# Sliding-window attention with experts on Trainium2: scores of two head pairs over 32 rows each, interleaved, and a block moved from behind the experts to the front

## Chip, cores and metric

One core of one Trainium2 chip runs the whole program. The metric is the device time of one execution in microseconds, the median of several runs.

## What is computed

The input x is 4 x 1024 tokens of 256 values, taken here as 32 blocks of 128 tokens. After a layer norm, three things are added to x: a gated mix of windowed and latent attention, a mixture of experts, and a shared expert.

```python
# per head (16 heads of 16): window of 128 keys behind each query
scores = einsum('bhnqd,bhnkd->bhnqk', qb, kb) * scale
attn = softmax(where(allowed, scores, NEG))
local = einsum('bhnqk,bhnkd->bhnqd', attn, vb)
# latent: 64 pooled tokens a batch, 4 heads of 16
lattn = softmax(where(lat_allowed, rq @ rk.T * lscale, NEG))
remote = (lattn @ rv) @ rout_w + rout_b
gate = sigmoid(local @ gl_w + remote_h @ gr_w)
attention = (gate * local + (1 - gate) * remote_h) @ out_w + out_b
# experts: top 8 of 64 for each token, and a shared one
y = sum_k w[k] * (silu(x @ We_gate[e_k]) * (x @ We_up[e_k])) @ We_down[e_k]
return x + attention + y + (silu(xn @ Ws_gate) * (xn @ Ws_up)) @ Ws_down
```

## The kernel before

Everything is float32, and the order on each engine is written out by hand; engines meet through counting semaphores only. The program runs in four stages: layer norm and routing; a first attention over blocks 0 to 16 (`FIRST` = 17); the experts, 96 pairs of tiles of 128 rows; and a second attention over blocks 17 to 31.

**One block of attention** is `body`, written once for each engine with eight steps `s` = 0 to 7, one for each pair of heads. In step s TensorE (PE) computes the scores of pair s (`scores`, line 824), transposes the probabilities of pair s-2 (`turn_probs`, line 838) and multiplies those of pair s-3 with the values (`values`, lines 850 to 852). VectorE (DVE) adds the mask, takes the minimum and writes the negated scores to `sm` (`mask_pair`, line 1544); ScalarE (ACT) takes the exponentials (`exps`, line 1116) and copies the transposed probabilities out of PSUM (`keep_prT`, line 1124). The other work is spread over the steps: projections (lines 771, 782, 784), the shared expert (792), the latent attention (`latent_scores` 858, `latent_turn` 864, `latent_values` 870), the gate (`mix_sums`, `mix`), and the output projection (811, 812). Steps of the block before (`tail`) are finished in the first steps of the next.

**Scores of a pair.** Queries lie transposed in `qT`, 8 heads of 16 rows on the 128 partitions of one half c. `keep_q` on DVE (line 1487) multiplies them by `own_head` and writes eight copies to `qz`, in each of which only one head's 16 rows are not zero. So the scores of a head come from a product over all 128 rows of `kT`:

```python
for u in range(2):
    last = mm(psS[:, p % 2, u * WIN:(u + 1) * WIN], qz[:, c, u, heads, :].rearrange("p h t -> p (h t)"),
              kT[:, c, u * UQ:u * UQ + WIN], start=True, stop=True)
```

One such product stands in the trace as two MATMUL and two LDWEIGHTS instructions. `psS` has two banks; pair p uses bank p % 2 and waits until DVE has masked pair p-2. `sm` and `pr` have four places, and `psT[:, 0]`, to which the probabilities are transposed, one: `turn_probs` waits for `keep_prT` of the pair before.

**The latent steps** of a block: PE `latent_scores` in step 4, DVE `latent_max` in step 5, ACT `latent_exp` in step 6 (ahead of `keep_prT` and `exps` of that step), PE `latent_turn`, ACT `keep_lprT`, PE `latent_values` in step 7.

**Scatter.** While the first attention runs, GpSimd (POOL) sends the normed rows of all 32 blocks to their experts' slots in DRAM: 256 indirect DMAs at line 636, in order, paced not to run ahead of PE. Before the experts begin, ACT waits for `attention(0, FIRST)` on its own queue and then for all of these to land; its first loads of expert rows are at line 1232.

**Combine.** In the second attention DVE also adds the experts' rows, 8 for a token, so 8 instructions at line 1604 for each of 32 blocks, each waiting for the one before (`combine`). Rows come in by DMA into four places (`rows_in`), of which SP refills one when its block is combined. Before: 16 adds in steps 4 to 7 of the first block behind (`resuming`), 16 in each of the other 14 (`combining`), 16 after the last block's steps (`closing`).

## Time and profile before

| | us |
|---|---|
| median of 3 runs | 1334.67 (1333.65 to 1336.95) |
| the profiled execution, its time | 1338.67 |
| its span in the profile | 1336.9 |
| PE busy | 1255.4 |
| DVE busy | 953.3 |
| ACT busy | 861.7 |
| POOL busy | 638.7 |

Of the span, routing takes about the first 105 us, the first attention from there to 478 us, the experts to 993 us, the second attention the rest. Times in rows are microseconds from the start of the span, durations of one instruction in groups are nanoseconds. What stands in square brackets behind a row is how long the engine was idle before it, and who released it. Ends of matmuls are modelled, and each lasts longer than the distance to the next: the work of PE is read from the distance between starts.

### The profile page before, as it was taken

The page shows a single profiled execution, that of the slowest core. Times are in us where ns is not written, and L with a number is a line of the kernel's source. Part 1 is how long each engine was busy: PE and PEld are TensorE (multiplying, and loading weights), DVE is VectorE, ACT ScalarE, POOL GpSimd, SP SyncE. Part 2 cuts the span into 40 slices and gives each one's busy share as a digit, 9 for nine tenths or more (in the row PEclk, how much of TensorE's full clock was granted, in tenths as well). Part 3 has the DMA queues.
Part 4 walks back from the last instruction along what each step waited for, and adds up shares of the span by engine and source line. Part 5 has one row for each costly group of instructions (what it writes and reads, how often), then busy time and mean ns, then how long its engine had stood idle before and what let it go on. Part 6 is the DMA issues. An engine that isn't in the chain of part 4 may idle for free.

```text
span 1336.9 us, 38681 instructions
## 1 busy us (share of the span) xinstructions
PE 1255.4 (94%) x9266; PEld 1182.4 (88%) x9267; DVE 953.3 (71%) x4532; ACT 861.7 (64%) x2383; POOL 638.7 (48%) x747
## 2 busy tenths in 40 slices
PE   4957999999999989999999999999999999999996
PEld 3956999999999979999999999999988999999985
DVE  6776666666666637667676676765559898989897
ACT  2323877777777856556565566566657777777774
POOL 7803777777777726565565665656650000000000
PEclk9678999999999979999999999999999999999998
DMA  8107455544333337777777777775545333333330
GB/s 255 63 1 280 163 185 188 206 163 162 123 118 112 114 120 223 211 233 223 224 232 212 233 226 214 233 215 170 175 139 218 107 106 106 106 109 113 116 119 19
DMA packets 152813, 218.40 MB, mean 163 GB/s; under 512 B 24769, under 2 KB 124866, under 8 KB 147650
## 3 DMA queue, kind: packets, MB, share of 16 engines
q1 hardware_dynamic: 80450, 86.77, 20.4%
q0 software_dynamic: 28800, 86.54, 16.9%
q10 hardware_dynamic: 43520, 44.57, 13.1%
q8 instruction: 19, 0.31, 0.1%
q14 instruction: 24, 0.20, 0.0%
HBM read 113.86 MB, written 103.81 MB: 163 GB/s over the span
## 4 chain that ended last, share of the span: by engine, by line
PE 73%; DVE 12%; issue 6%; DMA 3%; ACTq 2%; ACT 2%; DVEq 1%; SPq 1%
PE psS L951 19%; PE psS L824 10%; PE psT L935 5%; PE psO L960 5%; PE psT L838 4%; PE psM L960 4%; DVE x_all L1604 4%; DMA pr<-slot_rows 2%; PE psQ L771 2%; PE psV L811 2%; PE psV L782 2%; PE psQ L792 2%; PE psT L852 2%; PE psT L851 2%; PE psT L850 1%
## 5 line engine op out<-in xcount | busy, mean ns | idle before, releaser
L951 PEld LDWEIGHTS psS<-sm,wt 128*128 128x128 f32 x2560 | 310.8, 193 | 19.5 <-issue 7.8
L951 PE MATMUL psS<-sm,wt 128*128 128x128 f32 x2560 | 316.6, 277 | 1.7 <-ACT sm L1210 0.7
L636 POOL DMA_INDIRECT slot_rows<-x_out_st,idx_st x256 | 257.0, 1004 | 77.5 <-issue 68.6
L1116 ACT ACTIVATE pr<-sm,nmax 128x192 f32<-128x192 f32 x512 | 205.1, 449 | 54.5 <-DVE nmax L1544 52.7
L824 PE MATMUL psS<-kT,qz 128*128 128x192 f32 x1024 | 225.2, 343 | 10.8 <-DVE qz L1487 8.4
L663 POOL DMA_INDIRECT home_rows<-qz,row_idx x160 | 154.6, 966 | 131.0 <-DVE qz L1637 103.4
L663 POOL DMA_INDIRECT home_rows<-sm,row_idx x160 | 155.3, 971 | 86.4 <-issue 45.0
L1228 ACT COPY wt<-shared_mem 128x512 f32 x320 | 183.4, 627 | 4.8 <-issue 4.8
L1216 ACT ACTIVATE prT<-psS 128x256 f32<-128x256 f32 x160 | 61.6, 385 | 187.7 <-issue 100.0
L824 PEld LDWEIGHTS psS<-kT,qz 128*128 128x128 f32 x1024 | 164.3, 192 | 18.4 <-issue 10.3
L1544 DVE CUSTOM_DVE_ANT_0 sm<-psS,pr 128x192 f32<-128x192 f32 x512 | 162.0, 353 | 18.5 <-issue 14.6
L1124 ACT COPY prT<-psT 128x384 f32<-128x384 f32 x256 | 121.9, 476 | 77.6 <-PE psT L838 74.1
L1630 DVE TENSOR_TENSOR prT<-psS,prT 128x256 f32<-128x256 f32 x160 | 67.7, 423 | 105.3 <-ACT prT L1216 102.3
L838 PE MATMUL psT<-ident,pr 128*128 128x128 f32 x768 | 126.2, 273 | 1.3 <-ACT prT L1124 1.2
L1604 DVE SCALAR_TENSOR_TENSOR x_all<-shared_mem,w,x_all (+1 forms) x256 | 122.8, 480 | 1.1
L838 PEld LDWEIGHTS psT<-ident,pr 128*128 128x128 f32 x768 | 100.1, 142 | 7.7 <-issue 1.9
L1210 ACT COPY sm<-psT 128x512 f32<-128x512 f32 x160 | 93.6, 585 | 10.1 <-PE psT L935 5.4
L1542 DVE MEMSET met<- 1x1 f32 x256 | 15.1, 59 | 104.4 <-PE psS L824 93.8
L1487 DVE TENSOR_TENSOR qz<-qT,own_head 128x1024 f32<-128x1024 f32 x64 | 78.2, 1221 | 6.9 <-ACT qT L1050 6.9
L960 PE MATMUL psO<-shared_mem,prT 128*128 x320 | 82.4, 380 | 0.2 <-DVE prT L1630 0.2
L960 PE MATMUL psM<-shared_mem,prT 128*128 x320 | 82.3, 380 | 0.0
L935 PE MATMUL psT<-ident,pr 128*128 128x128 f32 x480 | 74.3, 279 | 4.4 <-DMA pr<-slot_rows 2.3
(283 smaller groups left out, 2492.6 us busy)
## 6 DMA issues: line engine op xcount, KB each, us to landing
shared_mem<-home_rows SPq DMA_DIRECT2D x32, 1024.0 KB, 5.1
pr<-slot_rows ACTq DMA_DIRECT2D x120, 272.0 KB
qz<-slot_rows ACTq DMA_DIRECT2D x40, 272.0 KB
slot_rows<-wt SPq DMA_DIRECT2D x32, 272.0 KB
shared_mem<-in_L_ffn_We_gate SPq DMA_DIRECT2D x64, 128.0 KB
shared_mem<-in_L_ffn_We_up SPq DMA_DIRECT2D x64, 128.0 KB
shared_mem<-in_L_ffn_We_down SPq DMA_DIRECT2D x64, 128.0 KB
x_all<-in_L_attn_x SPq DMA_DIRECT2D x4, 1024.0 KB, 9.1
```

Of the source, the lines that this page charges most:

```text
L636: pool.indirect_dma_start(slot_rows, bass.IndirectOffsetOnAxis(ap=idx_st[:, j, k:k + 1], axis=0), x_out_st[:, j % 2, :], None).then_inc(sc ...
L663: pool.indirect_dma_start(home_rows, bass.IndirectOffsetOnAxis(ap=row_idx[:, j, a:a + 1], axis=0), ys[j][:, a, :], None).then_inc(y_out[j] ...
L824: last = mm(psS[:, p % 2, u * WIN:(u + 1) * WIN], qz[:, c, u, heads, :].rearrange("p h t -> p (h t)"), kT[:, c, u * UQ:u * UQ + WIN], star ...
L838: last = nc.tensor.transpose(psT[:, 0, a * P:(a + 1) * P], flat[:, a * P:(a + 1) * P], ident[:])
L935: last = nc.tensor.transpose(psT[:, j % 2, (a * DC + c) * P:(a * DC + c + 1) * P], xs[j][:, a, c * P:(c + 1) * P], ident[:])
L951: last = mm(psS[:, j % 2, (2 * a + n) * P:(2 * a + n + 1) * P], wt[j % 2][:, a, c, n * F:(n + 1) * F], xsT[:, j % 2, a, c, :], start=(c == ...
L960: last = mm((psM, psO)[j % 2][:, a * D:(a + 1) * D], hT[:, j % 2, a, :], ring_d[:, e % RING, :], start=True, stop=True)
L1116: nc.scalar.activation(pr[:, p % 4, par, :], sm[:, p % 4, par, :], ACT.Exp, bias=nmax[:, p % 4, par:par + 1], scale=-1.0).then_inc(probs, 1)
L1124: nc.scalar.copy(prT[:, p % 2].rearrange("p a t -> p (a t)"), psT[:, 0, 0:3 * P]).then_inc(prT_ready, 1)
L1228: last = nc.scalar.copy(wt[j % 2][:, a, :, :], ring_gu[:, e % RING, :, :])
L1544: v.tensor_tensor_reduce(sm[:, p % 4, u, :], psS[:, p % 2, u * WIN:(u + 1) * WIN], mask[:, u * WIN:(u + 1) * WIN], -1.0, -FLOOR, ALU.add, ...
L1604: ins = v.scalar_tensor_tensor(x_all[:, t, :], row, w8[:, t, k:k + 1], x_all[:, t, :], ALU.mult, ALU.add)
```

## The change

1. **Scores.** In the first attention alone (`two = start == 0`), PE takes the scores of pairs s and s+1 together in each even step. Each product now runs over the 32 rows of its own pair. The order is: keys' half u = 0 of pair s, of pair s+1, then u = 1 of both; two neighbours have other rows of the array and another bank of `psS`. It waits until DVE has masked all pairs before s. DVE masks both in the even step.
2. **Queries.** `keep_q` writes two copies of 128 columns, by `own_half` (two sums on POOL before the first attention), in place of eight.
3. **Latent steps**, first attention alone: `latent_scores`, `latent_max`, `latent_exp`, `latent_turn` and `keep_lprT` one step sooner; `latent_values` stays in step 7, but ahead of `values`.
4. **Blocks.** `FIRST` is 18: 18 blocks in front of the experts, 14 behind. The adds of line 1604 are dealt out anew: 24 in steps 4 to 7 of the first block behind, 16 in each of the other 13, and 24 after the last block's steps (3 in each step).

```diff
-FIRST = NB // 2 + 1
+FIRST = NB // 2 + 2
...
+            after(nc.gpsimd.tensor_tensor(own_quarter[:], own_head[:, 0:4], own_head[:, 4:8], ALU.add))
+            after(nc.gpsimd.tensor_tensor(own_half[:], own_quarter[:, 0:2], own_quarter[:, 2:4], ALU.add))
...
+            def scores_of_two(i, p, nth):
+                n = i * NPAIR + p
+                c = p // PPC
+                if p % PPC == 0:
+                    pe.wait_ge(q_kept, DC * i + c + 1)
+                    pe.wait_ge(k_kept, DC * i + c + 1)
+                if p or nth:
+                    pe.wait_ge(masked, 2 * n)
+                for u in range(2):
+                    for m in (p, p + 1):
+                        r = slice(m % PPC * 2 * HD, (m % PPC + 1) * 2 * HD)
+                        last = mm(psS[:, m % 2, u * WIN:(u + 1) * WIN], qz[r, c, u, 0:2, :].rearrange("p h t -> p (h t)"),
+                                  kT[r, c, u * UQ:u * UQ + WIN], start=True, stop=True)
+                        if u == 1:
+                            last.then_inc(s_ready, 1)
...
-                    if live:
+                    if live and two and s % 2 == 0:
+                        scores_of_two(i, s, nth)
+                    if live and not two:
                         scores(i, s, nth)
...
-                    if s == 7 and live:
+                    if s == 7 and live and early:
+                        latent_values(i)
+                    if s == 7 - early and live:
                         latent_turn(i)
...
-                    if s == 4 and live:
+                    if s == 4 - early and live:
                         latent_scores(i, nth)
...
-                    if s == 6 and live:
+                    if s == 6 - early and live:
                         latent_exp(i, nth)
...
-                v.tensor_tensor(qz[:, c, :, :, :], bcast(qT[:, c, :].rearrange("p (u t) -> p u t", u=2), HPC, 2),
-                                bcast(bcast(own_head[:], UQ, 2), 2, 1), ALU.mult).then_inc(q_kept, 1)
+                n, own = (2, own_half) if two else (HPC, own_head)
+                v.tensor_tensor(qz[:, c, :, 0:n, :], bcast(qT[:, c, :].rearrange("p (u t) -> p u t", u=2), n, 2),
+                                bcast(bcast(own[:], UQ, 2), 2, 1), ALU.mult).then_inc(q_kept, 1)
...
-                    if live:
+                    if live and two and s % 2 == 0:
                         mask_pair(i, s, nth)
-                    if closing and s in (1, 2, 5, 7):
-                        n = (1, 2, 5, 7).index(s)
-                        if n == 0:
-                            dve.wait_ge(acc_done, NB - 1)
-                        combine(NB - 2 + n // 2, 2 + n // 2, range(n % 2 * 4, n % 2 * 4 + 4))
+                        mask_pair(i, s + 1, nth)
+                    if live and not two:
+                        mask_pair(i, s, nth)
+                    if closing:
+                        for n in range(3 * s, 3 * s + 3):
+                            if n == K:
+                                dve.wait_ge(acc_done, NB - 1)
+                            combine(NB - 3 + n // K, (NB - 3 + n // K) % ROWS, (n % K,))
...
-                    if s == 5 and live:
+                    if s == 5 - early and live:
                         latent_max(i, blk)
...
-                combine(2 * (i - FIRST) + n // K, 2 * ((i + 1) % 2) + n // K, (n % K,))
+                combine(2 * (i - FIRST) + 1 + n // K, 2 * ((i + n // K) % 2) + 1 - n // K, (n % K,))
```

**PE, loop of the first attention, steps 6 and 7.** In the rows that follow, ISA and REGISTER_ALU rows are addresses and waits. Before:

```order
L821 ISA
L824 MATMUL psS<-kT,qz 128x192 x2
L833 REGISTER_ALU
L838 MATMUL psT<-ident,pr 128x128 x3
L850 MATMUL psO<-v_mid,prT 128x72
L851 MATMUL psO<-va,prT 128x36
L852 MATMUL psO<-va,prT 128x36
L821 ISA
L824 MATMUL psS<-kT,qz 128x192 x2
L833 REGISTER_ALU
L838 MATMUL psT<-ident,pr 128x128 x3
L864 MATMUL psM<-ident,lpr 128x128 x2
```

and of the changed kernel, the same place:

```order
L839 ISA
L843 MATMUL psS<-kT,qz 128x192 x4
L853 REGISTER_ALU
L858 MATMUL psT<-ident,pr 128x128 x3
L884 MATMUL psM<-ident,lpr 128x128 x2
L870 MATMUL psT<-v_mid,prT 128x72
L871 MATMUL psT<-va,prT 128x36
L872 MATMUL psT<-va,prT 128x36
L853 ISA
L858 MATMUL psT<-ident,pr 128x128 x3
L890 ISA
L890 MATMUL psM<-rv,lprT 128x34
```

The two groups of scores are one of four products, and the latent transpose has moved from step 7 to step 6.

**ACT, loop of the first attention, steps 5 and 6.** `tz` is the gate's tanh. Before:

```order
L1044 COPY kT<-kT 128x128
L1124 COPY prT<-psT 128x384
L1115 ISA
L1116 ACTIVATE pr<-sm,nmax 128x192
L1115 REGISTER_ALU
L1116 ACTIVATE pr<-sm,nmax 128x192
L1095 ACTIVATE tz<-z 128x16
L1130 ACTIVATE lpr<-small 128x256
L1124 COPY prT<-psT 128x384
```

and now:

```order
L1070 COPY kT<-kT 128x128
L1156 ACTIVATE lpr<-small 128x256
L1150 COPY prT<-psT 128x384
L1141 ISA
L1142 ACTIVATE pr<-sm,nmax 128x192
L1141 REGISTER_ALU
L1142 ACTIVATE pr<-sm,nmax 128x192
L1121 ACTIVATE tz<-z 128x16
L1150 COPY prT<-psT 128x384
```

The latent exponential (`lpr`) stands ahead of the copy and the exponentials of step 5.

**DVE, end of the second attention.** `x_all<-psV` is the sum of a block's attention into x, `x_all<-shared_mem` the adds of experts' rows. Before:

```order
L1604 SCALAR_TENSOR_TENSOR x_all<-shared_mem,w,x_all 128x256
L1535 TENSOR_TENSOR x_all<-psV,x_all 128x256
L1604 SCALAR_TENSOR_TENSOR x_all<-shared_mem,w,x_all 128x256 x8
L1465 TENSOR_SCALAR den<-oa 128x16
L1467 RECIPROCAL rec<-den 128x16
L1469 TENSOR_TENSOR zl<-oa,rec 128x16
L1470 TENSOR_TENSOR small<-oa,rec 128x256
L1473 TENSOR_TENSOR z<-zl,remote_z 128x16
L1474 TENSOR_TENSOR dif<-small,remote_z 128x256
L1604 SCALAR_TENSOR_TENSOR x_all<-shared_mem,w,x_all 128x256 x4
L1479 SCALAR_TENSOR_TENSOR dif<-tz,dif 128x256
```

and now:

```order
L1640 SCALAR_TENSOR_TENSOR x_all<-shared_mem,w,x_all 128x256 x4
L1564 TENSOR_TENSOR x_all<-psV,x_all 128x256
L1640 SCALAR_TENSOR_TENSOR x_all<-shared_mem,w,x_all 128x256 x12
L1493 TENSOR_SCALAR den<-oa 128x16
L1495 RECIPROCAL rec<-den 128x16
L1497 TENSOR_TENSOR zl<-oa,rec 128x16
L1498 TENSOR_TENSOR small<-oa,rec 128x256
L1501 TENSOR_TENSOR z<-zl,remote_z 128x16
L1502 TENSOR_TENSOR dif<-small,remote_z 128x256
L1640 SCALAR_TENSOR_TENSOR x_all<-shared_mem,w,x_all 128x256 x6
L1507 SCALAR_TENSOR_TENSOR dif<-tz,dif 128x256
```

Three adds stand ahead of the sum, 12 in place of 8 between it and the gate's first half, 6 in place of 4 between its halves.

## Rows read from the trace of the kernel before

**Rows 1.** The page: busy time by engine, and the chain that ended last, by engine

```profile
PE 1255.4 (94%) x9266; PEld 1182.4 (88%) x9267; DVE 953.3 (71%) x4532; ACT 861.7 (64%) x2383; POOL 638.7 (48%) x747
...
PE 73%; DVE 12%; issue 6%; DMA 3%; ACTq 2%; ACT 2%; DVEq 1%; SPq 1%
```

**Rows 2.** Waits between 200 and 400 us: who <- whom, total, times, longest

```profile
DVE met L1542 <- PE psS L824: 51.1, 38, 1.6
...
ACT prT L1124 <- PE psT L838: 28.5, 30, 1.3
...
PEld psS L824 <- DVE nmax L1544: 2.9, 9, 0.3
...
PEld psM L870 <- issue: 2.1, 9, 0.2
```

**Rows 3.** Timeline of PE, latent scores of blocks 1, 16, 17, 31: start, us, ...

```profile
144.20 0.68 PE L858 MATMUL psM<-rkz,rqT 128*128 128x256 f32 x2
...
459.05 0.68 PE L858 MATMUL psM<-rkz,rqT 128*128 128x256 f32 x2
...
1006.86 0.68 PE L858 MATMUL psM<-rkz,rqT 128*128 128x256 f32 x2
...
1309.68 0.68 PE L858 MATMUL psM<-rkz,rqT 128*128 128x256 f32 x2
```

**Rows 4.** Timeline of PE inside one block of the front

```profile
299.73 0.91 PE L824 MATMUL psS<-kT,qz 128*128 128x192 f32 x4
300.48 0.49 PE L838 MATMUL psT<-ident,pr 128*128 128x128 f32 x3
...
310.47 0.90 PE L824 MATMUL psS<-kT,qz 128*128 128x192 f32 x4
311.20 0.49 PE L838 MATMUL psT<-ident,pr 128*128 128x128 f32 x3
...
316.07 0.82 PE L824 MATMUL psS<-kT,qz 128*128 128x192 f32 x4
316.72 0.49 PE L838 MATMUL psT<-ident,pr 128*128 128x128 f32 x3
```

**Rows 5.** Groups by line, 200 to 400 us: xcount | busy us, mean ns | idle

```profile
L824 PE MATMUL psS<-kT,qz 128*128 128x192 f32 x304 | 66.8, 342 | 0.9
...
L824 PEld LDWEIGHTS psS<-kT,qz 128*128 128x128 f32 x304 | 48.5, 191 | 3.5 <-DVE nmax L1544 2.9
...
L1487 DVE TENSOR_TENSOR qz<-qT,own_head 128x1024 f32<-128x1024 f32 x19 | 23.2, 1223 | 1.7 <-ACT qT L1050 1.7
```

**Rows 6.** Timeline of DVE and of ACT around the latent softmax of that block

```profile
312.20 0.17 DVE L1465 TENSOR_SCALAR den<-oa 128x16 f32<-128x16 f32 x1
...
313.70 0.35 DVE L1544 CUSTOM_DVE_ANT_0 sm<-psS,pr 128x192 f32<-128x192 f32 x1
...
314.26 0.41 DVE L1508 TENSOR_TENSOR small<-psM,lat_wide 128x256 f32<-128x256 f32 x1
...
315.62 0.42 ACT L1130 ACTIVATE lpr<-small 128x256 f32<-128x256 f32 x1 [0.37 <-DVE small L1513]
```

**Rows 7.** Line 636: its instructions (ns min/median/max), its group; ACT's first expert load

```profile
L636 POOL DMA_INDIRECT slot_rows<-x_out_st,idx_st x256: 954/960/2010, 130.5 to 470.1; - x128
...
L636 POOL DMA_INDIRECT slot_rows<-x_out_st,idx_st x256 | 257.0, 1004 | 77.5 <-issue 68.6
...
475.00 1.49 ACTq L1232 DMA_DIRECT2D pr<-slot_rows  x3
```

**Rows 8.** Timeline, first block behind (DVE, PE) and the last one (DVE)

```profile
1006.71 2.04 DVE L1604 SCALAR_TENSOR_TENSOR x_all<-shared_mem,w,x_all 128x256 f32<-128x256 f32 x4
...
1018.09 0.33 PE L876 MATMUL psM<-ident,lat 128*128 128x128 f32 x1 [1.62 <-DVE lat L1522]
...
1321.23 0.42 DVE L1535 TENSOR_TENSOR x_all<-psV,x_all 128x256 f32<-128x256 f32 x1 [2.28 <-PE psV L812]
1321.69 4.13 DVE L1604 SCALAR_TENSOR_TENSOR x_all<-shared_mem,w,x_all 128x256 f32<-128x256 f32 x8
```

More of the change, by code:

```diff
@@ L909, in body @@
                         project_qk(i + 1, 2)
-                    if s == 7 and live:
+                    if s == 7 and live and not early:
                         latent_values(i)
@@ L919, in attention @@
                     pe.wait_ge(ranks_kept, 1)
-                body(start, nth, tail=False, last_tail=False)
-                body(start + 1, max(nth, 1), last_tail=False)
+                two = start == 0
+                body(start, nth, tail=False, last_tail=False, two=two)
+                body(start + 1, max(nth, 1), last_tail=False, two=two)
                 with pe.Fori(start + 2, end - 1) as i:
-                    body(i, 2)
-                body(end - 1, 2, ahead=False)
+                    body(i, 2, two=two)
+                body(end - 1, 2, ahead=False, two=two)
                 body(end, 2, live=False)
@@ L1144, in keep_hs, with body @@
                 nc.scalar.copy(hsT[:], hs[:]).then_inc(hs_kept, 1)
-            def body(i, nth, live=True, tail=True, ahead=True):
+            def body(i, nth, live=True, tail=True, ahead=True, two=False):
+                early = 1 if two else 0
                 for s in range(NPAIR):
@@ L1197, in attention @@
                 keep_qk(start, 0, nth)
-                body(start, nth, tail=False)
-                body(start + 1, max(nth, 1))
+                two = start == 0
+                body(start, nth, tail=False, two=two)
+                body(start + 1, max(nth, 1), two=two)
                 with act.Fori(start + 2, end - 1) as i:
-                    body(i, 2)
-                body(end - 1, 2, ahead=False)
+                    body(i, 2, two=two)
+                body(end - 1, 2, ahead=False, two=two)
                 body(end, 2, live=False)
@@ L1608, in attention @@
                 nth = min(start, 2)
+                two = start == 0
                 if combining:
```

36 lines of the change are left out of this document (21 added, 15 removed).

## The prediction, made before the changed kernel ran

> **What bounds the kernel now.** I read the page first, then the waits of a stretch of each attention, then the timeline of single blocks. On the page PE is busy for 94% of the span and holds 73% of the chain of work that ended last [rows 1]. The waits of the front (the first attention) say who waits for whom: DVE waits for PE's scores 51.1 us in 200, ACT for PE's transposes 28.5 us, and PE for others almost nothing: 2.9 us for masks and 2.1 us ahead of the latent values [rows 2]. So the front runs at the pace of PE's work. DVE and ACT have some 5 and 3 us a block to spare.
>
> The pace of a block comes from the latent scores, one for each block [rows 3]: 15 blocks from 144.20 to 459.05, so 21.0 us a block in front; 14 blocks from 1006.86 to 1309.68, so 21.63 us behind. Behind, DVE adds experts' rows and the same PE work takes 0.6 us longer.
>
> What a pair's scores cost PE is the distance from their start to the next transpose: 0.75 and 0.73 us after short products, 0.65 us after long ones [rows 4]. I count six of the first kind and two of the second in a block: 5.7 us. A block has 21.0 us, less about 0.3 + 0.2 us idle (2.9 and 2.1 us in nine blocks [rows 2]), so 20.4 to 20.5 us of work, and 14.7 us of it are not scores.
>
> **The change, part by part.**
>
> *Scores of two pairs, called X.* Today 5.7 / 4 = 1.42 us. The four products are eight passes. Where PE streams, one pass takes 0.65 / 4 = 0.16 us, while the profile gives it 0.342 us from start to end [rows 4, 5]; the difference of 0.18 us is fill and drain, hidden today under the next pass. No row shows products over 32 rows, nor a change between those and products over 128. Bounds: from below 0.65 us, if the two pairs run wholly side by side and nothing is lost at the change; from above 1.46 + 2 x 0.18 = 1.82 us, if nothing overlaps and the pipeline is empty once before and once after. I take a value between: the two passes of one product lie on the same rows and must follow each other, while the second pass of one product and the first of the next lie on different rows. In order, eight passes then take five slots, 5 x 0.16 = 0.81 us, and with both ends exposed X = 0.81 + 0.36 = 1.17 us. The eight weight loads (0.191 us each [rows 5]) overlap one another already today, or four of them would not fit in 0.65 us, so I let them set nothing.
>
> The exposed ends speak against the change. The Trainium skill, "TensorEngine Tiling (Array Packing)", Key Properties, says that changing the tiling mode drains TensorE, which happens twice for each X here. If it holds, X is 1.17; were there no drain, X would be 0.81 and the block would meet the limits of the rival on full overlap below. The rule on overlap is in "TensorE: Matmul & The Clock Gate", Part 3: matmuls on different row groups run concurrently, while their order is kept. No row here can show either rule.
>
> *Waits in a block.* The 0.3 us for masks goes: today DVE is in the 1.22 us product of `keep_q` [rows 5] when pair 7's scores are ready; it now has a quarter of the columns (a 128x256 operation takes 0.41 us [rows 6]) and masks pair 7 before it. `latent_values` waited for ACT; with the turn a step sooner that goes too. A new wait is possible. `latent_exp` now stands ahead of `keep_prT` and `exps` of step 5, and PE's transpose in step 6 needs that copy. From the end of the scores of pairs 4 and 5, DVE masks two pairs (about 1.3: two spans like 313.70 to 314.26 with what lies around them), makes the gate sums (312.20 to 313.70, 1.5) and the latent maximum (314.26 to 315.62, 1.4) [rows 6]: 4.2 us. ACT then needs 0.42 for the exponential and some 0.4 for the copy: 5.0 us. PE arrives after 316.07 - 311.20 = 4.87, less 0.65 (scores of pair 5) and 0.5 (latent scores, moved), plus X: 4.9 us [rows 4]. So PE waits 0.1 us; I take 0.3 us a block for this and the like.
>
> *Front.* A block takes 14.7 + 4 x 1.17 + 0.3 = 19.7 us. 18 x 19.7 - 17 x 21.0 = 354.6 - 357.0 = **-2.4 us**.
>
> *Behind.* One block less: **-21.6 us**. Its 16 adds remain and go to the ends. In the first block DVE runs without a gap from the adds on and PE waits 1.62 us for it in the end [rows 8]; eight more adds at 2.04 / 4 = 0.51 us make **+4.1 us**. In the tail, three adds go ahead of the sum of block 30, into DVE's idle 2.28 us [rows 8]; between that sum and the gate stand 12 in place of 8, and between the gate's halves 6 in place of 4: 6 x 0.51 = **+3.1 us** on the only chain left. For both, nothing is the bound below (DVE has slack in the blocks after) and these figures the bound above; I take the full figures, because DVE has no gap at either place. The other blocks keep 16 adds.
>
> *Scatter.* 256 indirect DMAs run from 130.5 to 471.1 us, and ACT's first expert load comes at 475.0 [rows 7]. So the front can hardly end sooner than now: this covers whatever the scores win beyond some 3 us. The mean is 1004 ns and the median 960, with some up to 2010: were all at the median, the last would end 256 x 0.044 = 11 us sooner. A shorter `keep_q` may free some of that, if it is what disturbs them. The two sums for `own_half` lie on POOL's long start, and I cost them nothing.
>
> *Sum:* -2.4 - 21.6 + 4.1 + 3.1 = -16.8 us. The profiled execution took 1338.67 us (span 1336.9) and would take 1321.9; it lies 4.0 above the median of the runs, 1334.67, which becomes **1317.9 us**.
>
> **The rivals.**
>
> *A. No overlap, and a drain at each change (slower).* Eight passes one after another, 1.30 us, plus 0.36: X = 1.66. A block takes 14.7 + 6.64 + 0.3 = 21.6 us; 18 x 21.6 - 357 = +31.8, less 14.4 behind: +17.4 us, **1352 us**. It decides from X = 1.41 on: 18 blocks may take 357 + 14.4 = 371.4 us, 20.6 each, and (20.6 - 15.0) / 4 = 1.41, just what two pairs cost today. For it: in every matmul row here each pass follows the one before, and 8 mode changes a block are new. Against: weight loads run beside matmuls [rows 5], so the array does hold two things at once.
>
> *B. Nearly full overlap, stopped by the scatter.* With X near 0.65 PE could make a block in 18.0 us (14.7 + 2.6 and 0.7 of waits for ACT's order) to 18.6 us, and the front would be done 22 to 33 us sooner, but the scatters are not. The front then ends between 464 and 475 us in place of 475, and the total is 14.4 to 25.4 us below: **1309 to 1320 us**. For it: the 4 us between the last scatter and the first load. Against: it needs X well under 1.
>
> *C. The latent wait takes it all.* If DVE or ACT are 1 us later than reckoned above (two masks in a row ahead of sums and maximum; ACT stands still meanwhile), a block takes 20.7 us: 372.6 - 357.0 - 14.4 = +1 us, **1336 us**. For it: 4.9 against 5.0 us leaves nothing to spare. Against: ACT waits 28.5 us in 200 for PE today and could catch up.
>
> *D. The scores do not change* (32 rows treated as 128): X = 1.42, a block 20.7 us, the same **1336 us**.
>
> **How the numbers follow.** Forecast (X from 1.0 to 1.35): 0.50. A: 0.20. B: 0.20. C and D together: 0.10. About 0.3%, 4 us, is what a measurement here can tell from no change. Faster by more: forecast, B, and a little of C, 0.72; within: C and D, 0.08; slower: 0.20. The range holds B down to 1306 (its low end with the added DVE work behind costing somewhat less than I took) and reaches into A up to 1343 (X = 1.54), so about a tenth is left out above and less below.
>
> **What would show it.** In the changed kernel's timeline of PE, the distance from the first of eight score passes to the next transpose should be about 1.2 us (rival A 1.7, D 1.4, B under 0.9). The latent scores of blocks in front should stand 19.7 us apart, behind 21.6. The idle time ahead of PE's transpose in step 6 should be near 0.1 us, released by ACT; 1 us would be C. The last scatter should start at about 460 to 470 us and ACT's first expert load at 472; a wait of ACT there after the attention's end means B. The experts should keep their 514 us. The forecast is wrong if X is above 1.4, or if the adds dealt to the ends cost over 10 us.

## The result, and the profile after

| | before | after |
|---|---|---|
| median of 4 runs, us | 1334.16 (1333.12 to 1336.95) | 1321.01 (1318.75 to 1322.24) |
| the profiled execution | 1338.67 | 1318.75 |
| its span | 1336.9 | 1317.0 |

The changed kernel takes 0.9896 of the time of before, 95% interval 0.9876 to 0.9917: 13.2 us less, where 16.8 were forecast (1317.9 us). A second series, on another chip, gave 1321.0 us and 0.9908. Two of the experiments below, the ninth and the twelfth, fell on chips on which the kernel before itself took 1585 and 1564 us; they are read only where that leaves the rows comparable. The gain is shown only for chips on which before takes about 1334 us.

The page of the changed kernel: busy time by engine, the chain that ended last, and the group of the scatters (L640):

```profile
PE 1227.4 (93%) x9265; PEld 1130.0 (86%) x9267; DVE 925.1 (70%) x4532; ACT 854.2 (65%) x2383; POOL 634.3 (48%) x749
...
PE 70%; DVE 14%; issue 6%; DMA 4%; ACTq 2%; ACT 2%; DVEq 1%; SPq 0%
...
L640 POOL DMA_INDIRECT slot_rows<-x_out_st,idx_st x256 | 250.2, 977 | 77.5 <-issue 63.5
```

PE lost 28 us of busy time and still holds the chain. The scatters, which the change doesn't touch, have a mean of 977 ns in place of 1004 [rows 7].

The timeline of PE in one block of the front, the changed kernel:

```profile
296.44 0.92 PE L843 MATMUL psS<-kT,qz 32*128 32x192 f32 x8
297.47 0.52 PE L858 MATMUL psT<-ident,pr 128*128 128x128 f32 x3
...
306.50 0.92 PE L843 MATMUL psS<-kT,qz 32*128 32x192 f32 x8
307.35 0.55 PE L858 MATMUL psT<-ident,pr 128*128 128x128 f32 x3
...
311.08 0.92 PE L843 MATMUL psS<-kT,qz 32*128 32x192 f32 x8
311.93 0.55 PE L858 MATMUL psT<-ident,pr 128*128 128x128 f32 x3
...
316.04 0.92 PE L843 MATMUL psS<-kT,qz 32*128 32x192 f32 x8
```

Eight passes of two pairs now take 0.85 us from start to the next transpose, where one pair alone took 0.75 to 0.65 [rows 4]. A block is 316.04 - 296.44 = 19.60 us. Only in step 6 it is 1.03 (296.44 to 297.47): there PE waits some 0.18 us for ACT's copy, which stands behind the latent exponential.

The latent scores of blocks 0, 17, 18, 19 and 31 (the first two in front):

```profile
115.87 0.68 PE L878 MATMUL psM<-rkz,rqT 128*128 128x256 f32 x2
...
447.52 0.68 PE L878 MATMUL psM<-rkz,rqT 128*128 128x256 f32 x2
...
1000.30 0.68 PE L878 MATMUL psM<-rkz,rqT 128*128 128x256 f32 x2
...
1027.32 0.68 PE L878 MATMUL psM<-rkz,rqT 128*128 128x256 f32 x2
...
1287.95 0.68 PE L878 MATMUL psM<-rkz,rqT 128*128 128x256 f32 x2
```

In front (447.52 - 115.87) / 17 = 19.51 us a block, before 20.9 over all its blocks; behind, 12 blocks from 1027.32 on at 21.72, as before. The first block behind takes 27.0 us; it took 21.4.

Waits of the changed kernel between 200 and 400 us (columns as in [rows 2]):

```profile
DVE met L1571 <- PE psS L843: 53.3, 30, 3.2
...
ACT lpr L1156 <- DVE small L1542: 17.6, 10, 1.8
ACT prT L1150 <- PE psT L858: 17.3, 20, 1.4
```

ACT's new stall ahead of the latent exponential is there, 1.76 us a block, and took over part of the time in which ACT waited for PE (28.5 us before).

**Where the 19.9 us between the two spans lie**, by landmarks of both traces. Before started its first scores at 114.81, after at 107.69 us. The traces of the ten experiments on undisturbed chips have them between 105.9 and 109.4 us, the one with the scores of before among them (109.06). So about 6 of these 7 us belong to this one execution of before, which lies 4.5 us above its median. Without the first row of the table 12.8 us are left, beside the 13.2 between the medians.

| from ... to | before | after | difference |
|---|---|---|---|
| start to first scores | 114.81 | 107.69 | -7.1 |
| first scores to ACT's first expert load | 360.19 | 362.48 | +2.3 |
| to the first latent scores behind | 531.86 | 530.13 | -1.7 |
| to those of the last block | 302.82 (14) | 287.65 (13) | -15.2 |
| to the end | 27.22 | 29.05 | +1.8 |

The front with a block more costs 2.3 us, the part behind with one less gives 13.4.

ACT's queue where the front ends, in the timeline of the changed kernel:

```profile
469.95 0.37 ACT L1127 COPY mixedT<-psV 128x256 f32<-128x256 f32 x1 [1.60 <-PE psV L807]
470.17 1.49 ACTq L1260 DMA_DIRECT2D pr<-slot_rows  x3
```

and the scatters by their tile (ns min/median/max, first and last start):

```profile
L640 POOL DMA_INDIRECT slot_rows<-x_out_st,idx_st x256: 956/960/1214, 123.3 to 455.7; - x128
```

The load follows the attention's last copy at once, and the last scatter started 14 us earlier. So the front ends with PE's and ACT's work and not with the scatters; none of them now takes over 1214 ns, where the longest took 2010 [rows 7].

The last block of the front has a loss of its own. At 453.96 us PE has waited 1.82 us for ACT's copy (`prT`, L1150): in the other blocks the projections for the next block (L775, 314.08 to 316.04 in the block around the rows above) stand ahead of the scores of pairs 6 and 7, in the last there are none, and PE comes that much sooner. During the wait its granted clock falls to the lower of its two levels (0.62 on the mean of 452 to 457 us is 0.50 from 453.2 on). Stretches of 5 us (PE, PEld, DVE, ACT, POOL busy; granted clock, DMA share, GB/s):

```profile
447.00:452.00 5.00, 4.93 (x43) 4.10 (x42) 3.59 (x20) 3.73 (x13) 3.78 (x5) 1.00 0.30 111
452.00:457.00 5.00, 3.18 (x18) 3.07 (x16) 2.91 (x15) 3.08 (x9) 3.73 (x4) 0.62 0.30 111
457.00:462.00 5.00, 5.00 (x22) 4.63 (x21) 0.56 (x3) 2.94 (x10) 0.00 (x0) 0.50 0.08 28
```

0.50 is 1.2 GHz. The last block of before has 1.00 up to 473 us. PE works through from 453.96 to 463.4 us at half the clock (the product of L815 takes 1.71 us there from start to the next, 0.86 in the block around 302 us), which costs 4.7 us; of the wait, 1.6 us are beyond the 0.18 of an ordinary block. That makes **6.3 us**. A second count agrees: 18 blocks of 19.6 are 9.7 us short of the 362.5 of the front, 17 of 21.0 in the kernel before only 3.2 short of its 360.2, so 6.5 us more stand at the front's ends. It isn't the eighteenth block as such: with 17 blocks in front (the second experiment) the last one has the same wait,

```profile
436.67 0.87 PE L858 MATMUL psT<-ident,pr 128*128 128x128 f32 x3 [1.82 <-ACT prT L1150]
```

and the same fall of the clock.

### The profile page after: what moved, and what is told of

Read it like the earlier page. It is cut to its first block, busy times and chain, and to the rows that moved or that the text cites. A ratio compares the mean times of both kernels' runs of the same rounds, so it can differ in the third digit from the quotient of the medians.

```text
span 1317.0 us, 38599 instructions
## 1 busy us (share of the span) xinstructions
PE 1227.4 (93%) x9265; PEld 1130.0 (86%) x9267; DVE 925.1 (70%) x4532; ACT 854.2 (65%) x2383; POOL 634.3 (48%) x749
## 4 chain that ended last, share of the span: by engine, by line
PE 70%; DVE 14%; issue 6%; DMA 4%; ACTq 2%; ACT 2%; DVEq 1%; SPq 0%
PE psS L977 19%; PE psT L858 5%; PE psT L961 5%; PE psO L986 5%; PE psS L843 4%; DVE x_all L1640 4%; PE psM L986 4%; DMA pr<-slot_rows 3%; PE psQ L775 2%; PE psV L815 2%; PE psV L786 2%; PE psS L828 2%; PE psQ L796 2%; PE psT L872 2%; PE psT L871 2%
## 5 line engine op out<-in xcount | busy, mean ns | idle before, releaser
L640 POOL DMA_INDIRECT slot_rows<-x_out_st,idx_st x256 | 250.2, 977 | 77.5 <-issue 63.5
L1573 DVE CUSTOM_DVE_ANT_0 sm<-psS,pr 128x192 f32<-128x192 f32 x512 | 157.1, 354 | 19.3 <-issue 12.3
L1150 ACT COPY prT<-psT 128x384 f32<-128x384 f32 x256 | 121.8, 476 | 61.0 <-PE psT L858 58.5
L858 PE MATMUL psT<-ident,pr 128*128 128x128 f32 x768 | 133.4, 283 | 7.1 <-ACT prT L1150 4.2
L858 PEld LDWEIGHTS psT<-ident,pr 128*128 128x128 f32 x768 | 92.5, 147 | 28.7 <-issue 21.8
L828 PE MATMUL psS<-kT,qz 128*128 128x192 f32 x448 | 99.4, 346 | 2.8 <-DVE qz L1516 1.9
L828 PEld LDWEIGHTS psS<-kT,qz 128*128 128x128 f32 x448 | 72.6, 194 | 6.1 <-issue 3.2
L961 PE MATMUL psT<-ident,pr 128*128 128x128 f32 x480 | 73.2, 276 | 4.0 <-DMA pr<-slot_rows 2.8
L843 PE MATMUL psS<-kT,qz 32*128 32x192 f32 x576 | 67.0, 351 | 5.7 <-DVE qz L1516 5.7
```

The lines of the kernel that those rows point to most:

```text
L640: pool.indirect_dma_start(slot_rows, bass.IndirectOffsetOnAxis(ap=idx_st[:, j, k:k + 1], axis=0), x_out_st[:, j % 2, :], None).then_inc(sc ...
L858: last = nc.tensor.transpose(psT[:, 0, a * P:(a + 1) * P], flat[:, a * P:(a + 1) * P], ident[:])
L961: last = nc.tensor.transpose(psT[:, j % 2, (a * DC + c) * P:(a * DC + c + 1) * P], xs[j][:, a, c * P:(c + 1) * P], ident[:])
L1150: nc.scalar.copy(prT[:, p % 2].rearrange("p a t -> p (a t)"), psT[:, 0, 0:3 * P]).then_inc(prT_ready, 1)
L1573: v.tensor_tensor_reduce(sm[:, p % 4, u, :], psS[:, p % 2, u * WIN:(u + 1) * WIN], mask[:, u * WIN:(u + 1) * WIN], -1.0, -FLOOR, ALU.add, ...
```

## Experiments

All are measured against the kernel before, run on the same chip. "Block" is the mean distance of the latent scores in front, over all of them.

| | time, us | ratio to before | block | mean scatter, ns |
|---|---|---|---|---|
| before | 1334.2 | 1 | 20.89 | 1004 |
| the change | 1321.0 | 0.9896 [0.9876, 0.9917] | 19.51 | 977 |
| 11. the change again | 1321.0 | 0.9908 [0.9891, 0.9924] | 19.52 | 977 |
| 1. block and adds alone | 1341.1 | 1.0060 [1.0037, 1.0083] | 20.88 | 1004 |
| 2. without block and adds | 1322.6 | 0.9915 [0.9888, 0.9942] | 19.51 | 977 |
| 3. pair after pair | 1320.9 | 0.9906 [0.9876, 0.9935] | 19.52 | 977 |
| 4. joint, 128 rows | 1351.5 | 1.0135 [1.0086, 1.0185] | 21.54 | 1046 |
| 5. 32 rows, pairs apart | 1412.6 | 1.0585 [1.0533, 1.0636] | 24.82 | 974 |
| 6. behind too | 1331.6 | 0.9974 [0.9955, 0.9992] | 19.52 | 976 |
| 7. behind too, latent late | 1338.4 | 1.0001 [0.9960, 1.0041] | 19.51 | 979 |
| 8. latent late in front | 1334.5 | 0.9982 [0.9954, 1.0011] | 20.87 | 971 |
| 10. wide queries | 1336.5 | 1.0034 [1.0013, 1.0054] | 20.23 | 1030 |
| 9. wide queries (before: 1584.8) | 1599.9 | 1.0108 [1.0060, 1.0156] | | |
| 12. adds dealt otherwise (before: 1563.9) | 1570.3 | 1.0065 [1.0028, 1.0101] | | |

### 1 and 2: the two halves of the change

The first keeps the scores, queries and latent steps of before, with 18 blocks in front and the new adds:

```diff
-                two = start == 0
+                two = False
```

> Edit: the changed kernel with the first attention's scores, queries and latent steps as they were before; only the block is moved (18 in front, 14 behind) and the adds dealt out anew. Theory of the terms: one more block in front at 21.0 us, and behind the -13.3 us that the changed kernel's trace shows (one block less, the adds at both ends paid in full), so +7 to +8 us against the kernel before: 1341 to 1342 us. Rival (the move pays by itself, the gain is not of the scores): 1334 us or less.

The second has the new scores, queries and latent steps, with `FIRST` and the adds as before:

```diff
-FIRST = NB // 2 + 2
+FIRST = NB // 2 + 1
```

> Edit: the scores, queries and latent steps of the change with FIRST and the adds as before (17 blocks in front, 15 behind). Theory of the scatter as a floor: PE would end the first attention some 20 us sooner, but the last of 256 scatters starts about 340 us after block 0's latent scores, so ACT stands still ahead of its first expert load for 6 to 10 us and the whole is only 7 to 10 us below before: 1324 to 1327 us. Rival (no floor): the full 17 x 1.4 us come through, 1310 to 1313 us.

On their chip before took 1333.6 us. Moving the block alone cost 7.5 us, as theory had it; the other half alone won 11.1, 1 us more than theory's 7 to 10. The sum of the two, -3.6, is not the -13.2 of both. In the second, ACT's queue where the front ends:

```profile
452.47 0.37 ACT L1127 COPY mixedT<-psV 128x256 f32<-128x256 f32 x1 [1.60 <-PE psV L807]
460.29 1.49 ACTq L1260 DMA_DIRECT2D pr<-slot_rows  x3
```

The attention is done at 452.8 us and the first load waits until 460.29, for the last of the scatters, which starts at 457.7: 7.5 us lost. With 17 blocks this is the floor that the prediction spoke of. The eighteenth block fills the gap: it costs 19.6 us in front and 7.4 us of adds, and saves a block of 21.7 behind and the 7.5 us of standing, which leaves an estimate of 2 us won. The runs have 1322.6 against 1321.0 us, and their intervals overlap; so beside the new scores the move is worth about 2 us, which the runs can't tell from nothing, and nearly all of the 13.2 comes from the other half. By the same estimate the move would cost about 5 us if there were no floor.

### 3 and 4: what makes the eight passes short

The third exchanges the two loops, so that all products of one pair come ahead of those of the other, and no two neighbours but one lie on different rows:

```diff
-                for u in range(2):
-                    for m in (p, p + 1):
+                for m in (p, p + 1):
+                    for u in range(2):
```

> Edit: in the changed kernel the two loops of the joint scores are exchanged: both products of pair s, then both of pair s+1. Theory (products run side by side only with a direct neighbour on other rows): of eight passes only one or two overlap, X rises from 0.94 to about 1.4 us, 4 x 0.45 = 1.8 us a block, less what waits absorb: +20 to +30 us, 1341 to 1350 us. Rival (the array takes passes of free rows from further back in its queue, or passes are not bound by order): X stays near 0.95 us and the time at 1321 us.

The rival held: 1320.9 us, and the same distances. The eight passes of one group, by their single starts in the trace, with the last pass before and the transpose behind:

```
305.374 L872    305.583 L843    305.596 L843    305.850 L843    305.863 L843
306.012 L843    306.026 L843    306.175 L843    306.188 L843    306.440 L858
```

They start in twos, 13 ns apart, though in the program all four passes of pair p stand ahead of those of pair p+1, and both pairs' signals to DVE are carried by the last two. So PE takes passes for the other rows ahead of queued passes for the rows in use. The trace has no place in the queue for an instruction, but the signals tell it. In the interleaved order they belong to the sixth and the eighth pass; over 128 rows (the fourth experiment, the same loops) they stand at the sixth and the eighth; in the changed kernel, over 32 rows, at the seventh and the eighth, in twos 7 ns apart. So the overtaking happens in the changed kernel too. The two passes of one product don't overlap: in the fifth experiment, where a pair stands alone, its four passes start 0.267, 0.163 and 0.162 us apart. The interleaved order was not needed.

The same rows tell X apart. Eight passes are four slots; between twos lie 0.267, 0.162 and 0.163 us, the last two starts at 306.18, then 0.25 to the transpose. Against a slot of 0.163 the ends cost: 0.10 us before (305.374 to 305.583 is 0.21, and a pass of L872 follows its neighbour by 0.112), 0.10 at the first weight loads, 0.09 behind. X = 4 x 0.163 + 0.29 = 0.94 us.

The fourth keeps the joint order, but each product again runs over 128 rows, with eight copies of the queries:

```diff
-                        last = mm(psS[...], qz[r, c, u, 0:2, :]..., kT[r, c, u * UQ:u * UQ + WIN], ...)
+                        last = mm(psS[...], qz[:, c, u, heads, :]..., kT[:, c, u * UQ:u * UQ + WIN], ...)
...
-                n, own = (2, own_half) if two else (HPC, own_head)
+                n, own = HPC, own_head
```

> Edit: the changed kernel's order and waits, but each product over all 128 rows with the eight masked copies of the queries, as before the change. Theory (the gain is the passes side by side): X is 1.30 to 1.45 us, +0.4 to 0.5 us four times a block, less what waits absorb; 18 blocks give +20 to +32 us, 1341 to 1353 us, and scatters are back at a mean of about 1004 ns. Rival (the gain came from joint order, fewer waits and the earlier latent steps): within 5 us of 1321 us.

```profile
298.40 1.56 PE L843 MATMUL psS<-kT,qz 128*128 128x192 f32 x8 [0.66 <-DVE qz L1516]
299.80 0.49 PE L858 MATMUL psT<-ident,pr 128*128 128x128 f32 x3
...
309.86 1.46 PE L843 MATMUL psS<-kT,qz 128*128 128x192 f32 x8
311.15 0.49 PE L858 MATMUL psT<-ident,pr 128*128 128x128 f32 x3
```

Without the smaller row groups the same order takes 1.40 and 1.29 us, and the kernel is 30 us slower than the changed one. This run also has the wide queries; the tenth experiment differs from it in the 32 rows alone and takes 1336.5 us. So half of the 30 us, 15.0, is the rows' (21.54 for 20.23 us a block), and the other half the queries'. The joint order in itself wins nothing; and PE waits 0.66 us a block for the long `keep_q`, now that pair 0's scores come together with pair 1's.

### 5: 32 rows, but one pair at a time

```diff
-                two = start == 0
+                two = False
+                front[0] = start == 0
...
-                        scores(i, s, nth)
+                        scores(i, s, nth, front[0])
```

with `rows32` taking `kT` and `qz` over the pair's 32 rows, and two copies of the queries.

> Edit: e1 (block moved, order of steps as before the change), with each pair's scores in front over its own 32 rows from the two narrow copies, but each pair by itself in its own step: no neighbour on other rows. Theory (32 rows alone win nothing, each change between 128 and 32 rows costs about 0.1 us before and after): a pair's scores take 0.65 + 0.2 to 0.3 us in place of 0.71, eight times a block; less 0.3 us for the shorter query product: 18 blocks give +15 to +35 us on e1's 1341, so 1356 to 1376 us. Rival 1 (no cost of the change of rows): 1336 to 1341 us. Rival 2 (the two passes of one product run side by side on 32 rows, so no neighbour is needed): 0.33 us less a pair, 1310 to 1325 us.

```profile
301.62 0.91 PE L830 MATMUL psS<-kT,qz 32*128 32x192 f32 x4
302.47 0.55 PE L860 MATMUL psT<-ident,pr 128*128 128x128 f32 x3
```

Four passes of one pair take 0.85 us, exactly what eight passes of two pairs take. That is the ends' price: 8 times a block rather than 4, with no overlap to pay for it. From the last values before a group to the first behind its transposes it is 1.55 us (309.76 to 311.31), 1.28 in the kernel before (310.25 to 311.53): 0.27 us, 8 times 2.2 us a block. That is all by which undisturbed blocks are longer (23.2 us for 21.0), and over 18 blocks 40 us: 1381 us, already above the expected range. The 30 us that are left go with the granted clock and not with waits: busy time and clock in two stretches of 4 us of the front,

```profile
228.00:232.00 4.00, 4.00 (x30) 3.46 (x29) 1.84 (x11) 3.29 (x12) 3.08 (x4) 1.00 0.62 211
232.00:236.00 4.00, 4.00 (x16) 2.91 (x14) 2.03 (x11) 2.37 (x9) 3.08 (x4) 0.52 1.01 331
```

PE falls to its lower level for about 10 us every two blocks (0.92 on the mean of 150 to 440 us). It stood at 2.4 GHz with its records 100% busy until then, and its longest wait in a block is 0.12 us, so nothing in the waits announces it. Blocks with a fall take 27.4 us. Why the clock falls here and not in the changed kernel is not settled; both have 32 passes over 32 rows in a block, and this one spreads them over twice as many stretches.

### 6 and 7: the same behind the experts

```diff
-                two = start == 0
+                two = True
```

> Edit: the joint scores, narrow queries and early latent steps in the second attention too. Theory (behind, too, PE's work and not DVE sets the block): PE's work falls by 4 x 0.45 = 1.8 us, DVE's by 1.6 us for the two query products, and of 21.7 us a block 1 to 1.8 go: 14 blocks give -14 to -25 us, 1296 to 1307 us. Rival (behind, DVE's order sets it: the adds stand between masks and latent maximum, and ACT's latent exponential ahead of the copies of step 5 waits still longer for it): 1316 us or more.

The rival held: 10.5 us slower than the change, though PE has less work. Waits between 1040 and 1280 us:

```profile
ACT lpr L1156 <- DVE small L1542: 24.4, 11, 2.4
PEld psT L858 <- issue: 18.6, 54, 1.1
...
PE psT L858 <- ACT prT L1150: 6.4, 11, 0.8
```

Here DVE also adds experts' rows. It is late with the latent maximum, ACT stands 2.2 us a block ahead of the exponential, PE stands behind ACT, and its granted clock is 0.96 in this stretch (1.00 in the changed kernel). Not all of the loss lies in the blocks: the two profiled spans are 10.1 us apart, and 5.2 us are lost in the tail, from block 31's latent scores to the end (34.28 us for 29.05), where the clock stood at 0.50 twice, for 10.2 and 13.7 us. The seventh takes the latent steps behind late again:

```diff
-                early = 1 if two else 0
+                early = 1 if two == 1 else 0
```

> Edit: as e6, with the latent steps of the second attention where they were before. If the early latent exponential is what holds a block behind, this is faster than e6 by 5 us or more; if the place of the latent steps does not matter there, both agree within 3 us.

Inconclusive as to the order: ten executions range from 1321.5 to 1342.3 us. They follow the mean granted clock. Three at 0.958 or 0.959 took 1321.5 to 1326.3 us, seven at 0.945 to 0.947 took 1336.9 to 1342.3. In the profiled one, the slowest (1342.3 us), the blocks behind stand 23.9 us apart, and in each the clock falls for 6.8 us. In the sixth PE was busy for 219 of 240 us where the changed kernel has 233: with less work PE idles more, and what is won in work can be lost in clock. That the idle time is the cause is not shown.

### 8: latent steps late in front

```diff
-                early = 1 if two else 0
+                early = 0
```

> Edit: the changed kernel with the latent steps of the first attention where they were before. Theory (the early steps free PE of the 0.3 us ahead of the latent values, but give most of it back where the exponential waits for DVE): a block 0 to 0.5 us longer, 1321 to 1330 us. Rival (rival C of the prediction: the early exponential costs about 1 us a block): 1305 to 1315 us.

13.4 us slower than the change, beyond theory's range; the rival, which had it faster, is refuted. PE stands for the latent values,

```profile
227.98 0.63 PE L890 MATMUL psM<-rv,lprT 128*128 x4 [0.52 <-ACT lprT L1160]
```

and right after it runs at the low level, in stretches of 4 us:

```profile
226.00:230.00 4.00, 3.35 (x26) 2.95 (x25) 2.28 (x11) 3.61 (x13) 3.08 (x4) 0.88 0.61 198
230.00:234.00 4.00, 4.00 (x15) 3.04 (x12) 1.40 (x11) 2.19 (x8) 3.09 (x4) 0.50 1.00 326
```

Blocks without a fall are 20.3 us apart in place of 19.6, and twice in this front two blocks take 23.5 and 21.9. The wait can't be the whole cause of the fall: PE stands the same 0.52 us in the other blocks (at 187, 208 and 273 us, say), and the clock stays at 1.00. The profiled execution was the slowest of ten, 1339.67 us; the two at 1323.6 and 1323.8 us had the highest mean clock (0.975 and 0.978). So the earlier latent steps, which the prediction priced at the 0.2 us that PE waited, are worth on the median, beside the rest of the change, as much as the whole of it wins (13.2), in waits and clock together, and in the two fastest executions under 3 us; how that splits no trace of them shows.

### 9 to 11: the narrow queries

The changed kernel with eight copies of the queries again, products still over 32 rows:

```diff
-                n, own = (2, own_half) if two else (HPC, own_head)
+                n, own = HPC, own_head
```

> The changed kernel in all, but keep_q in the first attention writes eight copies of the queries again (a product of 1024 columns, 1.22 us, in place of 256), of which each product over 32 rows reads the two of its pair: PE's work and its order are those of the changed kernel. It tells what the narrow queries are worth beside the products over fewer rows. Theory: the long product of DVE is what lengthens the scatters, so their mean goes back from 977 to 1004 ns or more (the joint order with eight copies had 1046), the last one starts at 463 us or later in place of 455.7 and meets the end of the front (about 468), and PE waits again for masks of pair 7 and of pair 0, 0.3 to 1 us a block: 1324 to 1333 us. Rival: DVE has room, the scatters follow PE and not keep_q; then their mean stays at 977 to 985 ns, PE's block at 19.5 to 19.7 us, and the time is the changed kernel's within 3 us (1318 to 1324).

The ninth ran where before took 1585 us, this one 1600; in its front DVE stood up to 5.8 us at a time on a releaser outside the program's own engines, and it says nothing of the queries. The tenth is the same kernel and the eleventh the changed one, both on one undisturbed chip:

> The same kernel as in the run before (eight copies of the queries, products over 32 rows), again, because there the kernel before itself took 1585 us in place of 1334 and every DMA was slow. The expectations are those of that run: theory, scatters at a mean of 1004 ns or more, 1324 to 1333 us; rival, scatters at 977 to 985 ns, 1318 to 1324 us.

> The changed kernel itself, on the chip and in the hour of the run with eight copies, so that the two can be compared directly: 1319 to 1323 us if the kernel before takes 1334, scatters at a mean of 977 ns, 19.5 us a block in front. If the kernel before is slow here too, the difference between this one and the run with eight copies still tells theory (3 us or more) from rival (under 3 us).

1336.5 us against 1321.0 on the same chip: 15.5 us for `keep_q` alone, more than expected. The scatters' mean is 1030 ns, as theory had it, but that is not what costs. The last starts at 472.2 us and the first load comes at 482.91, directly behind the attention. A wait of PE between 200 and 400 us:

```profile
PE psS L844 <- DVE qz L1517: 6.5, 10, 0.7
```

and the group of `keep_q` there:

```profile
L1517 DVE TENSOR_TENSOR qz<-qT,own_head 128x1024 f32<-128x1024 f32 x20 | 24.4, 1220 | 2.6 <-ACT qT L1077 2.6
```

One `keep_q` takes 1.22 us (0.43 in the changed kernel). PE waits 0.65 us a block for the queries of pair 0, and the block is 0.71 us longer. The two profiled executions, the fastest of their kernels, are 11.8 us apart, and 11.4 of that lie between the first scores and the first load; the other 3.7 of the 15.5 us are in executions without a trace. So the narrow queries are no mere aid to the short products: without them all that the change wins is gone. The same holds on the median for the early latent steps (the eighth experiment); both keep PE from standing.

### 12: the adds dealt out otherwise

16 adds in the first block behind, 24 in the second, and the last 24 mostly behind the gate:

```diff
-                        for n in range(3):
-                            add_first_row(6 * s - 3 * NPAIR + n)
+                        for n in range(2):
+                            add_first_row(4 * s - 2 * NPAIR + n)
+                    if second:
+                        add_second_row(3 * s)
...
-                        for n in range(3 * s, 3 * s + 3):
+                        for n in range(sum(LAST_ADDS[:s]), sum(LAST_ADDS[:s + 1])):
...
+LAST_ADDS = (3, 2, 2, 2, 0, 1, 0, 14)
```

> The changed kernel in all, with the adds of experts' rows dealt out otherwise: 16 in place of 24 in the first block behind, 24 in place of 16 (3 in each step) in the second, and the last 24 put as 3, 2, 2, 2, 0, 1, 0 and 14 over the eight steps, so that 6 in place of 12 stand ahead of the gate, 1 in place of 6 between its halves, and 14 behind it. Theory: in the changed kernel DVE has no gap in the first block behind, which took 27.0 us in place of 21.4, and in the tail it finishes its adds early only to stand 2.80 us for the last output projection, having kept PE waiting 8.99 us for the gate. Then the first block behind comes back to 21.4 us (-5.6), the second takes 22.5 to 24 (its 8 more adds are 4.1 us and DVE has about 2.3 us of slack in a block), so +1 to +2.5, and the tail loses the 2.80 us less what the new order costs, -2 to -2.8: in all -5 to -7 us, 1314 to 1316 us. Rival: the 8 adds cost the same 5.6 us wherever they are put, and the end is set by DVE's sum of work: then only the tail's 2 to 2.8 us are won, 1318 to 1319 us, or nothing, 1321.

It ran where before took 1564 us (this one 1570), so the total is no answer to the question; it does say that on such a chip a variant of the change is 0.65% slower than before. The stage behind the experts, though, kept its pace there (21.7 us a block, as everywhere). The ninth, also on such a chip and with the adds of the change, has 317.2 us from block 18's latent scores to the end, the changed kernel 316.7 and 316.6. Latent scores of blocks 18, 19, 20 and 31:

```profile
1251.21 0.68 PE L879 MATMUL psM<-rkz,rqT 128*128 128x256 f32 x2
...
1274.18 0.68 PE L879 MATMUL psM<-rkz,rqT 128*128 128x256 f32 x2
...
1298.01 0.68 PE L879 MATMUL psM<-rkz,rqT 128*128 x2
...
1537.12 0.68 PE L879 MATMUL psM<-rkz,rqT 128*128 128x256 f32 x2
```

The first two blocks take 23.0 + 23.8 = 46.8 us, in the changed kernel 27.0 + 21.4 = 48.4. The tail, to the end of the span at 1563.7, takes 26.6 in place of 29.05. From block 18's latent scores to the end it is 312.5 in place of 316.7 us: **4.2 us less in this stage**, 2.4 of it in the tail, as the theory had it, but only 1.6 at the first blocks, where it had 3 to 4.6. Whether the whole kernel gains them, no run shows.

## Why the prediction was nearly right

The sign was right and the time is near (3.1 us off), but the branch that I called the forecast, X from 1.0 to 1.35, did not come: X is 0.94. By the table of landmarks 12.8 us are won and not 16.8. The front gave 4.7 us less than forecast and the part behind 1.0 less; the stage of the experts, for which I had nothing, gave 1.7 more, and that is chance: in the traces on undisturbed chips it lies between 528.5 and 532.7 us with the same code. The floor exists (the second experiment), but with 18 blocks it doesn't bind: 14 us lie between the last scatter's start and the load.

**X: 1.17 us forecast, 0.94 measured.** The step that failed is "eight passes then take five slots". It rested on passes being taken in the program's order, as the Trainium skill has it in "TensorE: Matmul & The Clock Gate", Part 3; the third experiment disagrees (starts 13 ns apart against that order), and so does the changed kernel, whose signals stand at the seventh and eighth pass. Both orders give four slots. Both ends together cost 0.29 us where I took 0.36. The Trainium skill's other rule, in "TensorEngine Tiling (Array Packing)", Key Properties, that a change of the tiling mode drains TensorE, agrees with this: the fifth experiment pays the ends with every pair (0.85 us for four passes, 0.65 to 0.75 over 128 rows). The sum needed only their size.

**Waits in a block: 0.3 us forecast, about 0.7 measured**, in the transposes of steps 5 and 6 and the values after them; ACT's stall behind DVE was foreseen, and came out at 1.8 us. With X at 0.94 the block should then be 14.7 + 3.8 + 0.7 = 19.2 us; it is 19.5 to 19.6. 0.2 us of the rest are the transposes behind the four groups, which take 0.38 us and not 0.33 to the next start. So the block's forecast, 19.7, was right by luck: X was 0.23 too high four times, and waits and gaps together 0.8 too low (0.2 of which I can't assign).

**Front: -2.4 us forecast, +2.3 measured.** What failed is "18 x 19.7": the last block of a front isn't like the others. In it PE waits 1.82 us and then runs at 1.2 GHz for a stretch, 6.3 us in all; the other blocks, 0.1 us shorter each than forecast, give 1.8 back. I had no term for the clock, anywhere; the fifth to eighth experiments show it to be a large risk of such a change.

**Behind.** A block less, -21.6 us, held. The 8 more adds in the first block cost 5.6 us and not 4.1: PE stood 1.53 and 1.52 us for DVE and ACT in it ([rows 8] had one such stand, 1.62), and its clock fell. The timeline of the changed kernel, with the adds around the first of them:

```profile
1006.27 1.52 DVE L1640 SCALAR_TENSOR_TENSOR x_all<-shared_mem,w,x_all 128x256 f32<-128x256 f32 x3
...
1010.18 1.07 PE L890 MATMUL psM<-rv,lprT 128*128 128x34 f32 x4 [1.53 <-ACT lprT L1160]
1010.85 1.39 DVE L1640 SCALAR_TENSOR_TENSOR x_all<-shared_mem,w,x_all 128x256 f32<-128x256 f32 x3
```

and its stretches after that, in which the granted clock of before is 1.00 at the same place:

```profile
1010.00:1015.00 5.00, 3.30 (x12) 2.81 (x13) 4.82 (x16) 2.42 (x9) 0.00 (x0) 0.50 0.66 211
1015.00:1020.00 5.00, 5.00 (x19) 4.52 (x20) 4.85 (x18) 2.97 (x11) 0.00 (x0) 0.52 0.67 223
```

The tail cost 1.8 and not 3.1:

```profile
1298.92 6.08 DVE L1640 SCALAR_TENSOR_TENSOR x_all<-shared_mem,w,x_all 128x256 f32<-128x256 f32 x12
...
1310.19 0.69 PE L807 MATMUL psV<-ident,small 128*128 128x128 f32 x2 [8.99 <-DVE small L1509]
...
1314.37 0.42 DVE L1564 TENSOR_TENSOR x_all<-psV,x_all 128x256 f32<-128x256 f32 x1 [2.80 <-PE psV L816]
```

PE waits 2.76 us longer for the gate than before (8.99 for 6.23), near the forecast, but the rest of the chain is a little shorter. The two places together, 7.4, meet the 7.2 forecast, and the first experiment, +7.5 us for the move alone, confirms it: a block costs about as much in front as behind, and the adds are the price.

**Scatter.** "A shorter `keep_q` may free some of that, if it is what disturbs them" is borne out: 977 ns with the short product, 1004, 1030 and 1046 in kernels with the long one (970 to 979 in the others with the short one). The same PE work with long and short product (the tenth and the eleventh) differs by 53 ns. What in the product does it isn't shown.

**The rivals.** A (no overlap) is refuted by 0.85 us. D (nothing changes) likewise. B comes nearest in X (its sign, "under 0.9" from start to transpose, is met by 0.85), but its block of 18.0 to 18.6 us did not come, and with 18 blocks neither did its floor, since the scatters ended early too; the 1321.0 us lie 1 us above its range. C had the right place, and a price of 0.4 us a block (0.7 for the 0.3 that I took) rather than 1. Of what would show it: the experts kept their time (520.8 us from load to the first scores behind, 522.5 before), and the adds at the ends stayed under 10 us.

## What to carry to other kernels

When the product that fills the array with zeros is cut to the rows it needs, count what else becomes smaller: here taking back the 32 rows costs 15.0 us (both with eight copies), and taking back the fewer copies 15.5. Products over separate row groups pay at every change of form, so gather them (two pairs in one stretch: 0.85 us, one pair alone: 0.85 us); their order inside the stretch doesn't matter. Before taking work off the bounding engine, ask what it will then wait for, since a waiting PE can lose clock as well as the wait, and look at the last block of a loop by itself: it lacks the work that fills the others' waits. When a stage is stopped by something else, work moved into it can use the gap, but the gain here was about 2 us and not clear of the noise.

## What was not expected of the hardware

- PE runs passes over other rows ahead of earlier ones in the queue: 13 ns apart in the third experiment, 7 ns in the changed kernel. Over 128 rows (the fourth) the signals keep the program's order.
- A short stand can cost more than itself: in the 1.82 us of waiting of the change's last front block the granted clock fell to 0.50 for 10.2 us. After a wait of 0.52 us in the eighth experiment it fell for 6.8 or 3.4 us in four of the 13 blocks between 150 and 440 us, and in the fifth it fell with no wait over 0.12 us; what decides is open.
- A long VectorE product lengthens GpSimd's indirect DMAs at the same time: 977 to 1030 ns on the mean of 256.
